# Dummy matmuls ahead of the loop, and layer 1's weights loaded and split later, in a two-layer feature-crossing kernel

## The reference

```
x0 = h = e                                   # [1024, 32, 64]
for layer in (0, 1):
    z = einsum('bhd,bmd->bhmd', h, x0)       # all products of a row of h with a row of x0
    out = relu(W[layer] @ z + b[layer])      # 128 rows out
    layer 0: h = out[:, :64]; out[:, 64:] is kept     layer 1: all 128 rows are kept
z = sum over the 64 numbers of the kept rows # [1024, 192]
y = relu(relu([z, dense] @ W_top1 + b) @ W_top2 + b) @ W_top3
```

## Time and profile before

| | us |
|---|---|
| median of 3 runs | 1962.54 (1962.13 to 1962.92) |
| the profiled execution | 1962.69 |
| its span, first to last instruction | 1960.9 |
| PE busy | 1929.4 |
| DVE busy | 1914.1 |
| POOL busy | 1826.8 |
| ACT busy | 1729.9 |

### The profile page before, as it was taken

One profiled execution on the slowest core, in us unless ns is written; L12 is line 12 of the kernel. 1 busy time (PEld: TensorE's weight loads), 2 busy tenths in 40 slices (PEclk: granted clock), 3 DMA queues, 4 the chain that ended last, 5 costly groups with the idle time before them and its releaser, 6 DMA issues.

```text
span 1960.9 us, 28730 instructions
## 1 busy us (share of the span) xinstructions
PE 1929.4 (98%) x7240; PEld 1361.7 (69%) x7240; DVE 1914.1 (98%) x1246; ACT 1729.9 (88%) x1959; POOL 1826.8 (93%) x646
## 2 busy tenths in 40 slices
PE   4999999999999999999999999999999999999999
PEld 2677767767777776776776776777777677677676
DVE  6999999999999999999999999999999999999995
ACT  4889989989988998998998999899899899889986
POOL 5999999999999999999999999999999999999883
PEclk9999999999999999999999999999999999999999
DMA  8988877777777777777777787787777787777730
GB/s 222 247 203 194 196 184 193 197 183 191 193 189 187 195 191 184 193 195 179 196 193 184 193 195 188 187 196 192 181 196 195 182 194 194 185 189 195 187 93 1
DMA packets 277281, 364.27 MB, mean 186 GB/s; under 512 B 116353, under 2 KB 116737, under 8 KB 277138
## 3 DMA queue, kind: packets, MB, share of 16 engines
q1 hardware_dynamic: 265058, 351.42, 72.5%
q0 software_dynamic: 8192, 8.40, 1.8%
q10 hardware_dynamic: 4016, 4.27, 0.8%
HBM read 347.02 MB, written 16.78 MB: 186 GB/s over the span
## 4 chain that ended last, share of the span: by engine, by line
PE 96%; DMA 1%; DVE 1%; POOL 1%; ACT 1%; issue 1%; ACTq 0%; DVEq 0%
PE out L825 22%; PE out L850 22%; PE out L844 21%; PE out L843 21%; PE out L833 7%; PE out L827 1%; POOL zl L319 1%; PE hrep L891 0%; DMA rot_low<-fields_dram 0%; ACT hrep L497 0%; ACT zh L484 0%; PE xr L891 0%; PE lz L891 0%; DVE zl L785 0%; DMA emb<-in_tables,idx 0%
## 5 line engine op out<-in xcount | busy, mean ns | idle before, releaser
L319 POOL TENSOR_TENSOR zl<-prod,zh 128x2048 fp32r<-128x2048 f32 (+2 forms) x384 | 1581.6, 4150 | 41.8 <-ACT zh L484 39.9
L843 PE MATMUL out<-zh,w1h 128*128 128x512 f32 x1888 | 736.5, 390 | 0.8 <-ACT relu L490 0.8
L844 PE MATMUL out<-zh,w1l 128*128 128x512 f32 x1888 | 736.6, 390 | 0.0
L484 ACT ACTIVATE zh<-prod 128x2048 fp32r<-128x2048 f32 (+2 forms) x384 | 664.8, 1731 | 20.4 <-DVE prod L730 10.2
L497 ACT ACTIVATE hrep<-out,b_sb 32x512 f32<-32x512 f32 (+1 forms) x768 | 496.3, 646 | 134.7 <-PE out L827 124.8
L850 PE MATMUL out<-zl,w1h 128*128 128x512 f32 x1888 | 565.9, 418 | 0.7 <-POOL zl L319 0.7
L825 PE MATMUL out<-prod,w_sb 128*128 128x512 f32 x1024 | 464.9, 597 | 27.5 <-DVE prod L661 22.6
L850 PEld LDWEIGHTS out<-zl,w1h 128*128 128x128 f32 x1888 | 354.4, 188 | 128.6 <-issue 61.5
L843 PEld LDWEIGHTS out<-zh,w1h 128*128 128x128 f32 x1888 | 354.7, 188 | 103.3 <-issue 30.4
L844 PEld LDWEIGHTS out<-zh,w1l 128*128 128x128 f32 x1888 | 354.4, 188 | 76.4
L825 PEld LDWEIGHTS out<-prod,w_sb 128*128 128x128 f32 x1024 | 195.3, 191 | 224.9 <-issue 215.0
(11 more groups left out here) (69 smaller groups left out, 723.1 us busy)
## 6 DMA issues: line engine op xcount, KB each, us to landing
rot_high<-fields_dram SPq DMA_DIRECT2D x510, 256.0 KB, 4.2
rot_low<-fields_dram SPq DMA_DIRECT2D x508, 256.0 KB, 6.2
xrep<-fields_dram SPq DMA_DIRECT2D x252, 128.0 KB, 2.6
left_x<-fields_dram SPq DMA_DIRECT2D x254, 64.0 KB, 2.2
left_y<-fields_dram SPq DMA_DIRECT2D x254, 64.0 KB, 2.2
fields_dram<-emb SPq DMA_DIRECT2D x504, 32.0 KB, 4.6
emb<-in_tables,idx POOLq DMA_INDIRECT x244, 3.5
w_sb<-in_w SPq DMA_DIRECT2D x1, 1024.0 KB, 6.3
```

What stands on the lines that cost most here:

```text
L319: pool.tensor_tensor(zl[u][:, 0:size, :], product[:, 0:size, :], zh[u][:, 0:size, :].bitcast(F32), ALU.subtract).then_inc(zl_made[u], 1)
L484: act.activation(zh[u][:, 0:size, :], product[:, 0:size, :], ACT.Copy).then_inc(zh_made[u], 1)
L843: nc.tensor.matmul(out1[:, :], w1h[:, k, :], zh[u][:, t, :], start=start and t == 0, stop=False)
L844: nc.tensor.matmul(out1[:, :], w1l[:, k, :], zh[u][:, t, :], start=False, stop=False)
```

## The change

`POOL` waits for step 1's rotations before it gathers block 2. `w1` is loaded behind SP's quarters of `rot_low[1]`. SP writes three groups of block 1 and loads all four quarters of `rot_high[0]`; ACT writes one group, and does so ahead of `copy_left(0)`. ACT rounds `w1` behind `finish_l0(0, 0, 0)`, DVE splits it within step 0, behind the first product into `z4`. PE runs four f32 matmuls (eight records) on operands that are there, into `out1`, ahead of `matmuls_l0(0, 0, 0)` and five (ten records) behind it; `out1` is overwritten by the first matmul of layer 1.

```diff
--- before.py
+++ after.py
@@ -351,6 +351,7 @@
                 if n >= 2:
                     pool.wait_ge(first_written, WRITTEN_APART)
                     pool.wait_ge(scratch_written[0], written(0, 1))
+                    pool.wait_ge(rot_low_loaded[1], 16 * QUADS)
                 for g in range(GATHERS):
                     gather(n % 2, known_rows(n), g)
             for c in range(BODY):
@@ -414,7 +415,6 @@
                     write_scratch(n, b, i + (c // 2 + AHEAD) // 2 + 1)
 
             sp.dma_start(ids_first_sb[:, :], ids_first).then_inc(ids_first_loaded, 16)
-            sp.dma_start(w1_sb[:, :, :], w1).then_inc(w1_loaded, 16)
             sp.dma_start(ids_sb[:, :], ids).then_inc(ids_loaded, 16)
             sp.dma_start(first_row_sb[:, :], first_row).then_inc(ids_loaded, 16)
             sp.wait_ge(first_gathered[0], 16)
@@ -425,9 +425,10 @@
             load_first_half(sp, SP_QUADS)
             sp.wait_ge(scratch_written[0], written(0, 1))
             load_second_half(sp, SP_QUADS)
+            sp.dma_start(w1_sb[:, :, :], w1).then_inc(w1_loaded, 16)
             sp.wait_ge(gathered[1], 16 * GATHERS)
-            write_groups(sp, 1, 1, (0, 1))
-            load_rotations(sp, 0, 1, SP_QUADS, rot_high[0], rot_high_loaded[0])
+            write_groups(sp, 1, 1, (0, 1, 2))
+            load_rotations(sp, 0, 1, QUAD_ORDER, rot_high[0], rot_high_loaded[0])
             sp.wait_ge(scratch_written[1], WRITTEN)
             sp.wait_ge(xr_copied, 2)
             load_xrep(1)
@@ -556,23 +557,22 @@
             load_first_half(act, ACT_QUADS)
             act.wait_ge(w0_folded, 4)
             act.activation(w0l_parts[:, :, :], w0l_sb[:, :, :], ACT.Copy).then_inc(w0l_rounded, 1)
-            act.wait_ge(w1_loaded, 16)
-            for u in range(PARTS):
-                act.activation(w1h[:, FIRST[u]:FIRST[u] + SIZES[u], :], w1_sb[:, SPLITS[u], :],
-                               ACT.Copy).then_inc(w1_rounded, 1)
             act.wait_ge(scratch_written[0], written(0, 1))
             load_second_half(act, ACT_QUADS)
             copy_x(0, 0)
+            act.wait_ge(gathered[1], 16 * GATHERS)
+            write_groups(act, 1, 1, (3,))
             copy_left(0)
-            act.wait_ge(gathered[1], 16 * GATHERS)
-            write_groups(act, 1, 1, (2, 3))
-            load_rotations(act, 0, 1, ACT_QUADS, rot_high[0], rot_high_loaded[0])
             round_left(0)
             copy_x(1, 1)
             act.wait_ge(bias_loaded, 32)
             replicate_h0(0)
             replicate_h1(0)
             finish_l0(0, 0, 0)
+            act.wait_ge(w1_loaded, 16)
+            for u in range(PARTS):
+                act.activation(w1h[:, FIRST[u]:FIRST[u] + SIZES[u], :], w1_sb[:, SPLITS[u], :],
+                               ACT.Copy).then_inc(w1_rounded, 1)
             for c in range(BODY):
                 step(0, c)
 
@@ -699,6 +699,13 @@
                 else:
                     dve.wait_ge(relu1_made, n * HALVES)
                     sum_rows(n, slice(0, P), slice(0, 1 + HALVES))
+
+            def split_w1():
+                for u in range(PARTS):
+                    part = slice(FIRST[u], FIRST[u] + SIZES[u])
+                    dve.wait_ge(w1_rounded, u + 1)
+                    nc.vector.tensor_tensor(w1l[:, part, :], w1_sb[:, SPLITS[u], :], w1h[:, part, :].bitcast(F32),
+                                            ALU.subtract).then_inc(w1_split, 1)
 
             def step(i, c):
                 m = i * BODY + c
@@ -724,6 +731,8 @@
                     dve.wait_ge(zl_made[4], m)
                 nc.vector.tensor_tensor(z4[:, :, :], repeated(hrep[1], 2), low[:, 0:2, :],
                                         ALU.mult).then_inc(z4_made[0], 1)
+                if known(m) and m == 0:
+                    split_w1()
                 dve.wait_ge(rot_high_loaded[b], (i * 2 + c // 2 + 1) * (16 * QUADS))
                 if later:
                     dve.wait_ge(zl_made[1], m)
@@ -756,11 +765,6 @@
                 rows = slice(q * FIELDS, (q + 1) * FIELDS)
                 nc.vector.tensor_tensor(w0l_parts[rows, :, :], w0l_sb[rows, :, :],
                                         w0l_parts[rows, :, :].bitcast(F32), ALU.subtract).then_inc(w0l_split, 1)
-            for u in range(PARTS):
-                part = slice(FIRST[u], FIRST[u] + SIZES[u])
-                dve.wait_ge(w1_rounded, u + 1)
-                nc.vector.tensor_tensor(w1l[:, part, :], w1_sb[:, SPLITS[u], :], w1h[:, part, :].bitcast(F32),
-                                        ALU.subtract).then_inc(w1_split, 1)
             products_l0(0, 0, 1)
             left_products(0)
             left_low(0)
@@ -875,7 +879,16 @@
 
             pe.wait_ge(w0_folded, 4)
             pe.wait_ge(w0l_split, 2)
+
+
+            def idle_work(times):
+                for _ in range(times):
+                    nc.tensor.matmul(out1[:, :], w0_sb[:, 0, :], feat0[:, 0:SC], start=True, stop=True)
+
+            pe.wait_ge(zeroed, 1)
+            idle_work(4)
             matmuls_l0(0, 0, 0)
+            idle_work(5)
             pe.wait_ge(w1_split, PARTS)
             for c in range(BODY):
                 step(0, c)
```

## The result

| | before | changed |
|---|---|---|
| median, us | 1962.59 (7 runs) | 1969.31 (7 runs, 1968.53 to 1971.14) |
| ratio to before, 95% interval | | 1.0035 (1.0025 to 1.0044) |
| span of the profiled execution, us | 1960.9 | 1967.5 |

The changed kernel is 6.7 us slower. I had forecast 1965.4 and a range to 1967.8, so the sign was right and the size was not.

What follows compares the result with a forecast made beforehand. PE was taken to bound the kernel, everything hanging on when it begins the loop's second `matmuls_l0`. PE's later start, +3.3, less a 0.45 POOL wait gave +2.8 on 1962.69, less 0.1 for the median: 1965.4 us, range 1962.3 to 1967.8.

Steps and rivals of the forecast that it cites:

- the sum by packet counts: DMA queues ahead of the loop: turns about equal by packet, `w1` mostly out first, 2.6 us; rotations land at 29.4.
- rival (b): Ahead of the loop, the `w1` load does not hold up the rotations: landing at 27.3, +0.7 us, 1963.3; chance 0.13.
- sum of +1 us: DMA queues: with turns of 9 to 17 descriptors, rotations land near 27.3 to 28, total about +1 us.
- (c): PE's second product: dummies keep the clock up, 2.1 us less; +0.7 us, or 1961.7 with early rotations; chance 0.10.
- (d): PE's second product starts past 38.5: +4 to +5.7 us, 1966.5 to 1968.2; chance 0.18.
- two mechanisms: For PE's late start: rotations landing past 30.5, or low clock through the whole second product, +1.5 us on the forecast.
- part 3: Step 0, weights rounded and split there: DVE's 5.53 us plus 2.43 of splits; PE begins at 37.4, 3.3 us later.

Runs made afterwards that it cites:

- experiment 1: Changed kernel with POOL's first L319 made to wait for the `w1` splits; 1965.84 us, ratio to before 1.0016.
- experiment 3: Changed kernel with `w1` loaded first and POOL's first L319 made to wait for the splits; 1964.01 us, ratio to before 1.0005.
- 5: Changed kernel with PE waiting for the splits behind the second first-layer product, no longer ahead of it; 1967.14 us, ratio to before 1.0023.
- 7: Changed kernel without POOL's wait for step 1's rotations, so block 2's gathers go out beside them; 1971.36 us, ratio to before 1.0043.
- experiment 2: Changed kernel with `w1` loaded first, as before the change; 1965.69 us, ratio to before 1.0013, ten times in two groups.
- 4: Changed kernel without the dummy matmuls on PE; 1969.49 us, ratio to before 1.0029, seven times in two groups.
- 6: Changed kernel with POOL's first L319 waiting for the splits and PE waiting for them behind the second product; 1965.44 us, ratio 1.0012.

## Why the prediction was wrong

**What held.** The loop's pace did not change. R, the landing of step 1's rotations, was forecast at 29.4: L664 started at 29.24 and waited for that DMA. That it agreed to 0.2 us was partly luck, since in the other profiles with the same order of loads L664 started at 29.92 to 31.07. T, the end of the first product, was forecast at 26.3 and came at 26.9. POOL's first L319 was forecast at 35.8 and came at 35.76. The idle stretch left the clock at the low level, and the second product took 5.8 us to layer 1 (41.56 to 47.38), as forecast. PE did not wait for POOL afterwards.

The load held up the rotations, as the sum by packet counts had it and rival (b) had not; experiments 1 and 3 price it at 1.8 us. This does not refute what the Trainium skill says on the page "DMA: Bandwidth & Descriptors", section "Queues, rings and completion order", of turns of typically 9 to 17 descriptors. If a packet of the profile is one descriptor, the 8 of `w1` on an engine fit into one such turn, and a turn of `w1` ahead of ACT's would delay the rotations too. So the prediction's step from larger turns to a sum of +1 us does not follow, and no run here tells the two kinds of turn apart.

Of the rivals, (b) and (c) did not occur. (d) had the right sign, and PE's start did move past 38.5, but by neither of its two mechanisms, and its 1966.5 to 1968.2 still lies below the 1969.3 measured.

**The step that failed** is in part 3: "and 2.43 us of splits: 7.96 us". I took 2.43 us from a row of 16.81 us, where POOL issued gathers, and moved it to 34.9, where by my own sum POOL's L319 starts at 35.8. The five splits took 6.72 us there. With 2.43 the second product would have begun at 29.24 + 7.96 = 37.2; it began at 41.56, 4.4 us later, 4.3 of them in the splits, and 1965.4 + 4.3 = 1969.7 against 1969.3 measured. Making POOL wait (experiment 1) gave 3.5 us of it back.

That L319 holds the splits is shown by experiment 1. That it is a lock and not a shared rate shows in four places. In all three profiles where L319 starts 1.0 us into the splits (the changed kernel, 5 and 7) they take 6.72 us, and in the five where it starts later (1, 2, 3, 4 and 6) 2.42 or 2.43. The held split ends just behind L319. In experiment 2 L319 in turn took 0.2 to 0.3 us longer where splits had come first; this is a single instance, and the profile's spans on POOL are rough. And where the order was open, the times fell into two groups some 4 to 5 us apart, which one added wait merged in the one case where that was tried.

What of the split makes it subject to the lock is read from rows, and no run varied it. DVE's other instructions read `hrep`, `xr`, `lz` or `z4` from PSUM and at most one tile from SBUF, and run at their usual 2.28 and 1.22 us beside L319 (L730 at 34.87 in the earlier trace rows beside L319 at 35.97 in the earlier trace rows, and all through the loop, where none of the 2.28 us kind took over 2.36); `w1_sb` and `w1h` both lie in SBUF. The Trainium skill, page "SBUF — State Buffer", section "Who interferes with whom", says just this: a DVE instruction with two SBUF inputs contends with a GpSimd instruction that reads SBUF, and which of the two starts first decides who blocks. The traces agree, with 4.85 us in place of 0.55. I had not looked for it, although it was the rule that spoke against the change.

**The sum, from the runs.** The change with `w1` left as before is 1961.6; splits and rounds in step 0 without the race add 2.4 (1964.0, experiment 3); the load behind the rotations 1.8 (1965.8, experiment 1); POOL's hold 3.5 (1969.3). These are differences of medians from different sets. In each of the three pairs no time of one kernel lies among those of the other, but the intervals of their ratios overlap, so the sizes are good to about 1 us. Forecast by terms were 2.4 for the splits, 2.1 for the load (29.4 against 27.3) and none for the hold.

## What to carry to other kernels

A duration belongs to its neighbours: before an instruction is moved, list what runs beside it at the new place, and for DVE whether both inputs lie in SBUF while POOL subtracts. Where two instructions exclude each other and their order is open, times can fall into groups, as in experiments 2 and 4; look at each run and not at the median alone, and put a wait where the order matters. A wait for a weight belongs directly ahead of its first use (2.2 us in experiment 5), and a lead won for one engine ahead of a loop is worth only what the other engines' start allows: of 4.4 and 4.1 us for PE at the third product, 1.5 and 1.9 were left at the seventh.

## What was not expected

- Letting POOL's four gathers run beside the rotations cost 2.0 us in the medians, though they move 128 KB and I had priced them at 0.5 to 0.9. The landings scatter by nearly as much, so the size is open.
- The lock seems to work both ways: L319 took 4.84 us in place of 4.54 to 4.63 in the one profile where it started in the middle of the splits and they went through. The loser appears to lose what is left of the winner's time.
- The dummies brought PE to the high clock at 21.8 us, within the first eight records, and the first product ran at 0.43 us a record; but PE then idled for 10.35 us, its clock fell at 35.5, within that stretch, and the gain went with it.
